# Pairwise interaction tower: plain fp32 matmuls of 64 rows in two row halves, in place of split fp32r operands

## The reference, cut to what matters

```python
B, N, E = 512, 40, 64                       # batch, fields, embedding size
e = stack([tbl_f[ids[:, f]] for f in range(40)], axis=1)      # (512, 40, 64), gathered rows
# one number for each of the 780 pairs i < j, in fp32:
#   z[b, (i,j)] = sum over f of (sum over e of x_i[b,e] * param[f,(i,j),e]) * x_j[b,f]
z = einsum('bie,fie,bif->bi', e[:, rowidx], param, e[:, colidx])
h = concatenate([z, dense_ctx], axis=1)     # (512, 780 + 16)
h = maximum(h @ W_top1 + b_top1, 0.0)       # 796 -> 512
h = maximum(h @ W_top2 + b_top2, 0.0)       # 512 -> 256
y = h @ W_top3                              # 256 -> 1
```

## Time and profile before

| | |
|---|---|
| Time, median of 3 runs | 625.62 us (625.51 to 630.67) |
| Span of the profiled execution | 626.6 us |
| PE busy | 339.2 us (54%), 1,484 instructions |
| PEld busy | 245.4 us (39%) |
| DVE busy | 375.5 us (60%), 457 instructions |
| ACT busy | 348.9 us (56%), 2,315 instructions |
| POOL busy | 305.2 us (49%), 266 instructions |

### The profile page before, as it was taken

One profiled execution on the slowest core, in us unless ns is written; L12 is line 12 of the kernel. 1 busy time (PEld: TensorE's weight loads), 2 busy tenths in 40 slices (PEclk: granted clock), 3 DMA queues, 4 the chain that ended last, 5 costly groups with the idle time before them and its releaser, 6 DMA issues.

```text
span 626.6 us, 6709 instructions
## 1 busy us (share of the span) xinstructions
PE 339.2 (54%) x1484; PEld 245.4 (39%) x1484; DVE 375.5 (60%) x457; ACT 348.9 (56%) x2315; POOL 305.2 (49%) x266
## 2 busy tenths in 40 slices
PE   0301010202020247687867787886888778897758
PEld 0201010201020136575755566664565445564523
DVE  0100010101111157999979999999999888887971
ACT  1100020002202137978897999889798897877762
POOL 6777777777777000000001356575574555663630
PEclk9999999999999959889789999989999899997868
DMA  6111111111112012211213223232231212322000
GB/s 185 36 27 39 26 41 26 43 26 26 27 45 47 2 42 58 74 36 40 76 52 80 66 56 88 83 93 65 66 102 36 75 39 76 77 69 79 18 1 0
DMA packets 19044, 33.52 MB, mean 53 GB/s; under 512 B 6687, under 2 KB 9503, under 8 KB 19004
## 3 DMA queue, kind: packets, MB, share of 16 engines
q1 hardware_dynamic: 13884, 27.84, 16.5%
q0 software_dynamic: 5120, 5.25, 4.2%
HBM read 33.08 MB, written 0.00 MB: 53 GB/s over the span
## 4 chain that ended last, share of the span: by engine, by line
another core or an unknown queue 28%; DVE 26%; ACT 15%; PE 14%; issue 11%; POOL 3%; DMA 2%; DVEq 0%; SPq 0%; ACTq 0%
ACT prod_s L587 12%; DVE z L504 7%; DVE prod_h L535 6%; DVE prod_s L535 6%; PE upsum L453 4%; PE upsum L454 4%; DVE prod_v L535 3%; POOL emb L355 2%; PE mpsum L404 2%; DMA w_raw<-param 2%; ACT w_high L564 1%; DVE w_low L291 1%; DVE x_parts L511 1%; PE mpsum L428 1%
## 5 line engine op out<-in xcount | busy, mean ns | idle before, releaser
L587 ACT ACTIVATE prod_s<-prod_s 128x64 f32<-128x64 f32 x1094 | 262.4, 242 | 143.9 <-DVE prod_s L535 86.8
L453 PE MATMUL upsum<-w_high,xT 128*128 128x512 f32 (+4 forms) x460 | 199.0, 438 | 55.8 <-DVE prod_s L535 16.1
L587 ACT ACTIVATION_READ_ACCUMULATOR prod_s<-prod_s 128x1 f32 x1094 | 205.6, 188 | 12.6 <-issue 12.6
L454 PE MATMUL upsum<-w_low,xT 128*128 128x512 f32 (+4 forms) x460 | 178.5, 394 | 0.0
L355 POOL DMA_INDIRECT emb<-tbl,rows_id x160 | 152.2, 951 | 50.2 <-issue 48.5
L291 POOL TENSOR_TENSOR w_low<-w_raw,w_high 128x1024 fp32r<-128x1024 f32 (+15 forms) x43 | 83.7, 1946 | 178.3 <-ACT w_high L564 178.3
L383 PE MATMUL tpsum<-ident,x_parts 128*128 128x128 f32 x156 | 30.7, 331 | 204.5 <-issue 103.6
L453 PEld LDWEIGHTS upsum<-w_high,xT 128*128 128x128 f32 x460 | 96.3, 209 | 102.2 <-issue 37.0
L535 DVE TENSOR_TENSOR prod_s<-upsum,emb 128x1024 f32<-128x1024 f32 (+4 forms) x75 | 84.1, 1121 | 86.3 <-remote 82.4
L535 DVE TENSOR_TENSOR prod_v<-upsum,emb 128x1024 f32<-128x1024 f32 (+4 forms) x59 | 66.0, 1118 | 86.4 <-remote 72.6
L383 PEld LDWEIGHTS tpsum<-ident,x_parts 128*128 128x128 f32 x156 | 22.3, 169 | 214.8 <-issue 111.0
(11 more groups left out here) (26 smaller groups left out, 98.6 us busy)
## 6 DMA issues: line engine op xcount, KB each, us to landing
w_raw<-param SPq DMA_DIRECT2D x64, 256.0 KB
emb<-tbl,rows_id POOLq DMA_INDIRECT x160
w<-W_top SPq DMA_DIRECT2D x1, 1536.0 KB
w_raw<-param SPq DMA_DIRECT2D x4, 240.0 KB
w_raw<-param SPq DMA_DIRECT2D x4, 224.0 KB
w_raw<-param SPq DMA_DIRECT2D x4, 208.0 KB
w_raw<-param SPq DMA_DIRECT2D x4, 192.0 KB
w_raw<-param SPq DMA_DIRECT2D x4, 176.0 KB
```

The source lines that it names most:

```text
L453: pe.matmul(tile, x, w_high[:, w % W_SLOTS, cols], start=True, stop=False)
L454: last = pe.matmul(tile, x, w_low[:, w % W_SLOTS, cols], start=False, stop=True)
L587: last = act.activation(ring[:, at:at + E], ring[:, at:at + E], ACT.Copy, accum_out=z[:, d["c0"] + r, d["pair"] + q:d["pair"] + q + 1])
```

## The change

The operands are no longer split. `x_parts`, `w_raw`, `w_high`, `w_low`, their semaphores and all instructions that make them (L302, L511, L564, L291) are gone. The matmuls take plain fp32 operands over 64 rows. A plain fp32 matmul stands in the trace as two loads of weights and two MATMULs.

- *Couples.* Two fields, 2k and 2k+1, are a couple. One turn of 128 columns (`turn_x`, L353) puts field 2k on rows 0 to 63 and field 2k+1 on rows 64 to 127 of `xT`; the parameters are laid out by the host in the same halves, so that one DMA (L292) brings the weights of a couple, up to 2,496 columns. 20 couples in place of 39 fields.
- *Units.* A unit is now one block of the batch by up to 16 pairs, or, up to eight pairs, two blocks by the pairs: 230 units, the same 199,680 columns, 460 matmuls of up to 512 columns. Units of the two halves alternate, and PE issues them in pairs: first bank of one, first bank of the other, second bank of one, second bank of the other (`fill`, L434).
- *Shares.* vector 85 units with 72,256 columns, pool 53 with 50,624, tensor 39 with 35,008, scalar 53 with 41,792. Pool units begin at unit 130. The first sum on PE stands behind unit 9.
- *z in the order of work.* z is numbered as the units come, the dense columns first, and the host sorts the rows of `W_top1` alike. Groups become ready from 0 upward. Group ends are units 43, 84, 118, 151, 185, 225 and 229; groups 5 and 6 are done after the units (`LATE`).
- *PSUM.* `abank` takes the turns of x, of z and the first layer, all emptied by ACT in one order; `vbank` takes the sums.
- *The turn of a couple* is placed at the couple's own first unit for the first ten couples, and six units ahead for the others.

With `PASSES = 1` all gathers are issued at the start as before, in the order of the couples (field 39, 38, 37, ...).

The diff, cut to its core:

```diff
-D_LAG = 4
-H_LAG = 4
+V_LAG = 1
+H_LAG = 3
 ...
-SHARES = [(0, 0.4, 0.16, 0), (76, 0.31, 0.12, 0.4), (176, 0.34, 0, 0.45)]
-LOW_BY_POOL = (65, 1.0)
+SHARES = [(0, 0.24, 0.2, 0.0), (130, 0.17, 0.16, 0.55)]
 ...
+            for t in range(max(len(c) for c in chunks)):
+                now = [c[t] for c in chunks if t < len(c)]
 ...
+                for c in range(s * per, (s + 1) * per):
+                    for half, i, j, n in now:
+                        two = per > 1 and n * E <= BANK
+                        if two and (c - s * per) % 2:
+                            continue
 ...
+    for q in range(1, NQ):
+        back = 0 if q < COUPLES // 2 else TURN_BACK
+        place(max(couples[q]["first"] - back, couples[q - 1]["first"] + (1 if back else 0)), ("x", q, 0))
+    LATE = []
+    for s in range(PASSES):
+        at = 0
+        for g in range(G):
+            at = max(at, group_end(s, g) + 8)
+            if s + 1 == PASSES and at >= NU - 8:
+                LATE.append(g)
+            else:
+                at = place(at, ("group", s, g))
 ...
+            for m in range(M1):
+                at = place(at, ("part", s, m))
 ...
-                for lo in (0, E):
-                    sp.dma_start(w_raw[lo:lo + E, s, 0:n * E],
-                                 param[:, at:at + n, :].rearrange("e q f -> e (q f)")).then_inc(raw_in[s], 16)
+                sp.dma_start(w[:, q % W_SLOTS, 0:width(q)], param[:, at:at + width(q)]).then_inc(w_in[q % W_SLOTS], 16)
 ...
+            def turn_x(q):
+                s, k = couples[q]["s"], couples[q]["k"]
+                pe.wait_ge(gathered[q], 16 * 2 * PER)
+                take_abank()
+                for c in range(PER):
+                    last = pe.transpose(abank[:, c * P:(c + 1) * P],
+                                        emb[:, s * PER + c, 2 * k:2 * k + 2, :].rearrange("p i e -> p (i e)"), ident[:])
+                last.then_inc(abank_full, 1)
 ...
-                    pe.matmul(tile, x, w_high[:, w % W_SLOTS, cols], start=True, stop=False)
-                    last = pe.matmul(tile, x, w_low[:, w % W_SLOTS, cols], start=False, stop=True)
+                    last = pe.matmul(upsum[u % U_TILES][:, bank, 0:hi - lo],
+                                     xT[rows, d["q"] % X_SLOTS, (c % PER) * P:(c % PER + 1) * P],
+                                     w[rows, d["q"] % W_SLOTS, d["w"] + lo:d["w"] + hi], start=True, stop=True)
 ...
+                for bank in (0, 1):
+                    for v in now:
+                        if bank == 0:
+                            begin(v)
+                        fill(v, bank)
```

592 lines of the change are left out of this document (285 added, 307 removed).

## The result

The changed kernel takes 674.4 us (median of 4 executions, 669.5 to 688.0), the kernel before beside it 628.1 us: a ratio of 1.068, 95% interval 1.059 to 1.077. The predicted time was 638 us (600 to 720), slower with 60 in 100.

What follows compares the result with a forecast made beforehand. DVE was taken to bound the main stage, after a slow start limited by late word of PE's results. 228.6 + 336 + 17 + 20 + 37.6 = 639 us, less 1.0: 638 us, range 600 to 720.

Steps and rivals of the forecast that it cites:

- A: Whole kernel: slow start stays, DVE bounds, boundaries and tail eat the split's gain; 605 to 665 us, 50 in 100.
- B: Main stage: PE bounds because the two row halves don't overlap, 4.4 us a pair; 703 us, 22 in 100.
- Slow start: First stage: stays 228.6 us at 1.40 us per instruction, ending in the fourth couple, 3,840 to 7,168 columns done.
- DVE's work: Main stage: 352.0 us busy, less 44 for split operands, plus 28 for added work, gives 336 us.
- DVE's idle time in the main stage: Main stage: 17 us of waits at couple boundaries plus 20 us of other idle time.
- PE per pair: Main stage: with halves overlapped, 1.8 us of fills plus 0.9 of sums and turns, 2.7 against DVE's 3.6.
- The clock: Main stage: about 53 us at the lower clock level, costing up to 14 us, counted in the range only.
- Boundaries: After 228.6 us, four couples following a scalar unit: DVE idles 4.2 us each around the turn's copy, 17 us.
- Tail: End of kernel: 20 first-layer products move behind the last fill; 37.6 us in place of 19.2.
- Rival C: First stage: the change ends the slow start, so only gathers and DVE count; 463 us, 15 in 100.
- The early sums: First stage: sums on PE, 45 us each at the slow step, lengthen it; 650 to 680 us, 5 in 100.

Runs made afterwards that it cites:

- halves apart: Changed kernel with both banks of one unit filled, then both of the next, in place of alternating: 497.6 us, ratio 1.001 to the kernel before.

## Why the prediction was right, and where it was not

The verdict and the mechanism (A: slow start stays, boundaries and tail eat what the split gave back) came out; the time was 36 us short of the median. At 674.4 us the result lies outside A's own range of 605 to 665 and inside the whole range only by the room that it gives to B and to a longer start, neither of which came. A's range was also narrower than its own terms: 638 + 14 + 18.5 + 6 is 676.5. By the steps of the sum, against the profiled execution:

- **Slow start**, 228.6 us, fourth couple: measured 230.1, with the four couples of 7,168 columns just done. Right, to 1.40 us per instruction. What I could not know from one trace is that other chips don't show it.
- **DVE's work**, 336 us: measured 331.8. Right.
- **DVE's idle time in the main stage**, 17 + 20 = 37 us: measured 75.2. This is the step that failed, and two terms under it did. *PE per pair*: I put 1.8 us for the fills at full overlap, and 2.7 with sums and turns, well under DVE's 3.6. Measured at the full clock: 2.55 for the fills, 0.84 for sums, 3.5 in all. PE did not need less than DVE but as much; only about half of the overlap was had. *The clock*: I allowed 53 us at the lower level, at 0.27 us each, up to 14 us, and left it out of the sum. Measured: 75.2 us at 0.45 each, 34 us. At the full clock's rate (0.10 of 407 us) DVE would have been idle for 41 us, near the 37 of the sum, so it is through the clock that the first error shows. With 6.3 us of PE work a pair at the lower clock, measured, in place of 4.9, my own formula gives 1 - 3.6/6.3 = 0.43, an estimate next to the 0.45.
- **Boundaries**, 4 x 4.2 = 17 us: PE waited 14.7 us for xT in five waits. The waits were there, the longest 6.8; taking them away brought 6 us, and 10 to 14 in the kernel with the turns from the sixth couple on and the halves apart (481.0 and 484.2 at 0.957 and 0.958, to 494.6).
- **Tail**, 37.6 us: measured 49.0 in the profiled execution, in which 20 us of it ran at the lower clock, and 39.2 at the full clock (halves apart, last reduction at 452.7 of 491.9 us). Right for the full clock. Timeline of PE in the first trace, the block of products and what follows:

```profile
637.89 4.53 PE L374 MATMUL abank<-zT,w 128*128 128x512 f32 x10 [0.93 <-ACT h L541]
643.29 4.53 PE L374 MATMUL abank<-zT,w 128*128 128x512 f32 x10 [0.87 <-ACT h L541]
648.69 4.53 PE L374 MATMUL abank<-zT,w 128*128 128x512 f32 x10 [0.87 <-ACT h L541]
656.77 15.65 PE L374 MATMUL upsum<-zT,w 128*128 128x512 f32 x16 [0.68 <-ACT zT L539]
672.35 9.79 PE L472 MATMUL upsum<-h,w 128*128 128x512 f32 x16
```

  A quarter of the products every 5.4 us, as estimated; the last product block takes 15.7 us here and 8.5 at the full clock.

Sum of the deviations: +1.5 - 4.2 + 38.2 + 11.4 = 47 us, from 639 to 686.1. Of these some 44 are the lower clock (34 in the main stage, 10 in the tail), the term that I had left out of the sum. The other three executions were 12 to 19 us shorter, at clocks of 0.911 to 0.964 for 0.888; but the shortest, 669.5 us, is the one at 0.911, so on this chip the mean clock of the whole span doesn't order them.

- **Rival B** (PE bounds, no overlap, 703 us): false in its premise, but its verdict on PE was half right. Its own case, run, took 161 us over the changed kernel (on another chip) where 703 - 638 = 65 was said. Its price per pair was right, 4.5 us at the full clock for 4.4; what it left out is the lower clock, 96 us at 9.0 a pair, and that without the slow start PE is the bound from the first couples on.
- **Rival C** (no slow start, 463 us): not in the comparison that was predicted, but on three of four chips. Its sum of 463 carries the same missing 38 us of idle time, and the measured times were 494 to 521 us. I had asked whether the change would end the slow start, not whether the chip would.
- **The early sums** (the rest, 650 to 680 us) were said to lengthen the slow start. They didn't: it ended at 230.1 us. That the result lies in this range is chance.
- **The other drawback of the kernel before**, the stall behind POOL's gathers, is in no step, because the only trace hid it.

## What to carry to other kernels

A stage that is limited by something outside the kernel hides the waits behind it, so a change that is judged on one chip may be judged on that cover: here the same two programs stand at 1.07 on one chip and at 1.00 (1.02 by the medians) on another. When an engine's work per unit comes out below the bounding engine's only if everything overlaps, count what the buffers allow (here, by an untested reading, two free tiles out of three), and price the lower clock with the engine's real share: at level load each microsecond of it cost 0.45. And relieving the engine that stands level with the bound (sums to an ACT that was 27% busy, turns ahead, halves apart) brought 7% where the exchange of the matmul form alone brought nothing.

## What was not expected of the hardware

- On one chip of four (and in the first comparison, whose chip isn't known) word of PE's and ACT's results arrives at 1.40 us per instruction for the first 230 us, on three others not at all, with the same programs, 160 gathers of 945 ns at the same pace. The cause stays open; the gathers alone are not it.
- MATMULs of 64 rows in one half start beside those of the other half (0.01 us apart) even where four of the latter stand ahead of them in program order, and the order within a pair did not matter for the time (497.6 us; ratio to the kernel before 1.001, for the changed kernel's 1.000).
- Two row halves give 1.86 times the rate of one (1.99 us for 3.70), and in one half a MATMUL of 64 rows and 512 columns takes 0.46 us, no less than one of 128 rows in the products (0.45 us: 4.53 us for 10).
- Going from sums over 128 rows to plain fp32 fills over 64 rows, or back, costs PE 0.2 us at the full clock (0.205 + 0.53 for 0.11 + 0.43); into fp32r fills over 128 rows it costs nothing (0.03 + 0.31 for 0.11 + 0.23).
